# Transposing by the whole array in even head steps and by two row tiles in odd ones, with the weighted sum turned back three steps late

## The chip, the cores and the metric

One core of a Trainium2 chip runs the whole program. Its engines are PE (TensorE: MATMUL, and PEld for its weight loads), DVE (VectorE), ACT (ScalarE), POOL (GpSimd) and SP (SyncE, which issues the DMAs). The metric is the device time of one execution in microseconds (us), lower being better; the median of three runs is taken.

## What is computed

The program has six stages over 128 rows of 256 numbers, each added to a residual behind a layer norm. The change lies in the first, a cross attention over 12544 context rows with 16 heads of 64:

```python
q = x1 @ Wq
kv = x2 @ Wkv
k, v = jnp.split(kv, 2, axis=-1)
...
attn = jnp.einsum('bhid,bhjd->bhij', q, k) * SCALE
attn = jax.nn.softmax(attn, axis=-1)
out = jnp.einsum('bhij,bhjd->bhid', attn, v)
...
return out @ Wo + bo
```

The other stages (a banded attention, a mixture of 8 experts, a cross attention with relu keys, a state scan, and a mixture of 32 experts) stay as they are.

## The kernel before, in words

`stage_context` goes over the context in 14 chunks of 896 rows (`CK`, seven blocks of 128), and in each over 16 heads: 224 head steps `u`, in one loop on every engine. The order of the work is written out by hand, engine by engine, and held together by semaphores; each engine runs its own list in order. Keys and values are never stored whole: they are projected as the heads need them. Products that must be exact are split in a high and a low part (`Kh`, `Kl`; `cTh`, `cTl`), and three products of the parts are summed.

What PE does in step `u`, in this order (lines of the kernel before):

1. waits for the exponential of step u (`exp_done`), for `pTl_ready` of step u-1 and for `u_added`, and transposes the 128x896 tile `prob` into `pT_ps`, banks 4 and 5 of PSUM (L669 to L673). It works in two row tiles: rows 0 to 63 of `prob` go through one half of the array into bank 4, rows 64 to 127 through the other half into bank 5, with 14 transposes of 64 rows, two at a time;
2. from u = 2 on, `turn_sums(u - 2)` (L598 to L602): waits until DVE has added the two halves of the weighted sum into `osb` (`o_added`) and transposes it, again in two row tiles, into columns 448 to 511 of the banks 4 and 5 (`O_ps`), and signals `p_turned`;
3. in odd steps, `scores` (L587 to L596) of the next two heads: 12 matmuls in two row tiles, since a head has 64 numbers;
4. in steps of `v_steps` (all but u % 8 = 6, and not the last eight), `values` (L577 to L585): 6 matmuls of 128x512 into bank 6, for the values of a later group of heads. In six of the last eight steps `later_keys` stands in their place (keys of stage four);
5. `piece(u + 4)` (L563 to L575): 6 matmuls of 128x448 into bank 7, half the keys of a pair of heads, four steps ahead. It waits for `kl_ready` of the piece before;
6. `weighted_sum(u - 1)` (L604 to L618): 7 matmuls of 128x256 into bank 6 (`OT_ps`), with the values as weights and the high and low parts of the transposed probabilities as moving data.

All in 3, where it runs, and in 1 and 2 works by row tiles; all in 4 to 6 works by the whole array.

ACT copies `pT_ps` to the high part of `pT` (L427), copies the values (L435), forms the exponential of step u+1 (L402, L404) and copies the keys (`Kh`, L395). DVE subtracts for the low parts (L525 for `pT`, L463 for `Kl`), takes the maxima of the scores (L470), adds the turned sum to `U` (`update_sums`, L485, behind `p_turned`), updates `den` (L533) and adds the two halves of the weighted sum (`add_parts`, L478, behind `pv_done`), in this order:

```python
if u >= 2:
    update_sums(u - 2)
...
if u >= 1:
    add_parts(u - 1)
```

POOL splits the values, SP loads a chunk every 16 steps. Behind the last step the rest of the sums is turned, scaled (`scale_sums`), transposed by `turn_heads` (L633, whole array) and multiplied with `Wo` (L638).

The transposes of `norm_tensor` (L115) and those of `stage_relu_context` (L1359) work by the whole array too.

Of the kernel before, what the change touches and what calls it, by code (L numbers as in the profile page):

```python
# [17 lines left out]
F32 = mybir.dt.float32  # L18
# [4 lines left out]
ALU = mybir.AluOpType  # L23
# [3 lines left out]
P = 128  # L27
# [153 lines left out]
def stage_context(nc, t, sb, sem, link, ps, norms, v):  # L181
# [17 lines left out]
    with ExitStack() as keep:  # L199
# [12 lines left out]
        pT = [sb(f"pT{i}", [P, NT, 2, P], F32R, keep) for i in range(2)]  # L212
        osb = sb("osb", [P, P], F32, keep)
        nm = sb("nm", [P, 2, H0], F32, keep)
# [19 lines left out]
        pT_ps = ps[:, 4:6, 0:HK].rearrange("p s (t q) -> p s t q", q=P // 2)  # L234
        O_ps = ps[:, 4:6, HK:512]
        OT_ps = ps[:, 6, 0:2 * P]
        halves = (slice(0, DH0), slice(DH0, P))
# [20 lines left out]
        def v_low(g, i):  # L258

            return V[g % 2][:, i, :, DH0:P]  # L260

        def by_row(x):

            return x.rearrange("p t (s q) -> p s t q", s=2)
# [5 lines left out]
        with nc.Block() as block:  # L270
# [111 lines left out]
            def _(act):  # L382
# [70 lines left out]
            def _(dve):  # L453
# [22 lines left out]
                def add_parts(u):  # L476
                    dve.wait_ge(sem("pv_done"), u + 1)
                    nc.vector.tensor_reduce(osb[:, :], OT_ps.rearrange("p (a q) -> p q a", a=2), AX_X,  # L478
                                            ALU.add).then_inc(sem("o_added"), 1)
# [40 lines left out]
                for u in range(steps):  # L520
                    h, b = u % H0, u % 8
                    if 1 <= u and u - 1 + AHEAD < steps:
                        low_parts(u - 1 + AHEAD)
                    dve.wait_ge(sem("pTh_ready"), u + 1)
                    nc.vector.tensor_tensor(by_row(pT[u % 2][:, :, 1, :]), pT_ps,  # L525
                                            by_row(pT[u % 2][:, :, 0, :]).bitcast(F32), ALU.subtract).then_inc(sem("pTl_ready"), 1)
# [10 lines left out]
                    if u >= 1:  # L537
                        add_parts(u - 1)
                    if u >= steps - H0 + 3 and u % 2 == 1:
                        scale_sums((u - (steps - H0) - 3) // 2)  # L540
                update_sums(steps - 2)
# [7 lines left out]
            def _(pe):  # L549
# [48 lines left out]
                def turn_sums(u):  # L598
                    pe.wait_ge(sem("o_added"), u + 1)
                    for s, rows in enumerate(halves):  # L600
                        mm = nc.tensor.transpose(O_ps[:, s, :], osb[rows, :], ident[rows, rows])  # L601
                    return mm  # L602

                def weighted_sum(u):  # L604
                    h, g = u % H0, u // HG
                    pe.wait_ge(sem("pTl_ready"), u + 1)
                    if u >= 1:
                        pe.wait_ge(sem("o_added"), u)
# [53 lines left out]
                for u in range(steps):  # L662
                    h, g = u % H0, u // HG
                    pe.wait_ge(sem("exp_done"), u + 1)
                    if u >= 1:
                        pe.wait_ge(sem("pTl_ready"), u)
                    if u >= 3:
                        pe.wait_ge(sem("u_added"), u - 2)
                    for k in range(NT):  # L669
                        for s, rows in enumerate(halves):  # L670
                            mm = nc.tensor.transpose(pT_ps[:, s, k, :],  # L671
                                                     prob[:, :, :].rearrange("p a n -> p (a n)")[rows, k * P:(k + 1) * P],
                                                     ident[rows, rows])  # L673
                    if u >= 2:
                        mm = turn_sums(u - 2)
                    mm.then_inc(sem("p_turned"), 1)
                    if u % 2 == 1 and u + 1 < steps:
                        pe.wait_ge(sem("kl_ready"), u + 3)
                        scores((u + 1) // 2)
                    if u in v_steps:  # L680
                        j = v_steps.index(u)
                        gn, i = g + 1, V_AT.index(u % HG)
                        if j == 0:
                            pe.wait_ge(sem("first_vl"), NT)
                        else:
                            pe.wait_ge(sem("vraw_ready"), j)
                        if u >= 2:
# [16 lines left out]
                    if u >= 1:  # L704
                        if u in v_steps:
                            pe.wait_ge(sem("vraw_ready"), v_steps.index(u) + 1)
                        if u in later_at:
                            pe.wait_ge(sem("dkT_ready"), later_at.index(u) + 1)
                        weighted_sum(u - 1)
                    if u == steps - 1:  # L710
# [1172 lines left out]
```

## Time and profile before

| | |
|---|---|
| median of 3 runs | 1496.01 us (1495.39 to 1496.62) |
| the profiled execution | 1500.16 us |
| its span, first to last instruction | 1498.3 us |
| mean granted clock of TensorE | 0.983 of 2.4 GHz |
| PE busy | 1442.7 us, 96% |
| PEld busy | 1228.0 us, 82% |
| DVE busy | 1070.5 us, 71% |
| ACT busy | 827.8 us, 55% |
| POOL busy | 607.0 us, 41% |

The profile is of one execution. Busy time is the union of an engine's instructions; matmuls are pipelined, and their ends are modelled, so one matmul's row overlaps the next one's, and starts say more than ends. A row of a timeline gives start, length of the whole group, engine, line, operation, what is written and read, the shapes and how many instructions; in brackets how long the engine had stood idle, and for what. Head steps of `stage_context` run from 31.7 to 1143 us, three quarters of the whole span.

### The profile page before, as it was taken

What the parts mean: (1) busy time and instruction counts of PE and PEld (TensorE: products, weight loads), DVE (VectorE), ACT (ScalarE), POOL (GpSimd) and SP (SyncE); (2) the same over time, 40 slices, a digit from 0 to 9 for tenths busy, and PEclk for the clock granted to TensorE, in tenths of its full rate; (3) what the DMA queues carried; (4) which work ended last, traced back from release to release, by engine and by line L of the source; (5) the groups of instructions that cost most, each with busy time, mean ns of one, the idle gap of its engine ahead of it and who ended that gap; (6) DMA issues with size and microseconds to landing.
All of it is one profiled execution on the core that took longest, in us unless ns stands there. A gap on an engine that the chain in (4) does not pass through costs nothing. (4 is left out here: it accounts for less than half of the span.)

```text
span 1498.3 us, 28535 instructions
## 1 busy us (share of the span) xinstructions
PE 1442.7 (96%) x11057; PEld 1228.0 (82%) x11057; DVE 1070.5 (71%) x2051; ACT 827.8 (55%) x1578; POOL 607.0 (41%) x524
## 2 busy tenths in 40 slices
PE   8999999999999999999999999999998889999678
PEld 7888888888888888888888888888886879998558
DVE  5777777777777777777777777777785646677774
ACT  4666666666656666666666666666662236666221
POOL 4353434435343435353434343443420327765330
PEclk9999999999999999999999999999999799999889
DMA  5000000000000000000000000000013502111810
GB/s 190 2 25 2 1 26 1 26 1 26 1 26 1 26 2 26 2 26 2 26 2 25 2 6 21 1 26 1 1 54 132 200 23 87 56 59 35 340 74 4
DMA packets 11257, 59.41 MB, mean 40 GB/s; under 512 B 2346, under 2 KB 4723, under 8 KB 10100
## 3 DMA queue, kind: packets, MB, share of 16 engines
q1 hardware_dynamic: 11124, 57.59, 10.4%
q8 instruction: 89, 1.46, 0.4%
q14 instruction: 44, 0.36, 0.1%
HBM read 57.45 MB, written 0.13 MB: 38 GB/s over the span
## 5 line engine op out<-in xcount | busy, mean ns | idle before, releaser
L525 DVE TENSOR_TENSOR pT<-ps,pT 128x896 fp32r<-128x896 f32 x224 | 244.5, 1092 | 174.7 <-ACT pT L427 174.7
L344 POOL CAST V<-Vraw 128x512 fp32r<-128x512 f32 x189 | 115.5, 611 | 619.0 <-ACT Vraw L435 515.5
L427 ACT ACTIVATE pT<-ps 128x896 fp32r<-128x896 f32 x224 | 206.0, 920 | 152.3 <-PE ps L601 152.0
L435 ACT COPY Vraw<-ps 128x512 f32<-128x512 f32 x189 | 110.8, 586 | 263.8 <-PE ps L582 263.8
L345 POOL TENSOR_TENSOR V<-Vraw,V 128x512 fp32r<-128x512 f32 x189 | 242.2, 1281 | 15.1
L470 DVE TENSOR_REDUCE nmx<-ps 128x1 f32<-128x896 f32 x224 | 242.1, 1081 | 0.0
L615 PEld LDWEIGHTS ps<-pT,V 128*128 128x128 f32 x1568 | 215.8, 189 | 10.7 <-ACT d_kT L411 2.4
L404 ACT ACTIVATE prob<-ps,nm 128x896 f32<-128x896 f32 x224 | 224.2, 1001 | 0.0
L615 PE MATMUL ps<-pT,V 128*128 128x256 f32 x1568 | 221.1, 280 | 1.4 <-ACT d_kT L411 1.4
L478 DVE TENSOR_REDUCE osb<-ps 128x128 f32<-128x256 f32 x224 | 95.1, 424 | 101.0 <-PE ps L615 99.3
L671 PE MATMUL ps<-ident,prob 64*128 64x64 f32 x3136 | 145.8, 230 | 4.1 <-ACT prob L404 2.6
L582 PE MATMUL ps<-wvh,cTh 128*128 128x512 f32 x392 | 143.2, 446 | 1.2 <-DVE V L515 1.2
L671 PEld LDWEIGHTS ps<-ident,prob 64*128 64x128 f32 x3136 | 115.2, 139 | 34.6 <-ACT prob L404 5.3
L463 DVE TENSOR_TENSOR Kl<-ps,Kh 128x448 fp32r<-128x448 f32 x224 | 137.6, 615 | 1.8 <-ACT Kh L395 1.8
L571 PE MATMUL ps<-cTh,wkh 128*128 128x448 f32 x448 | 130.8, 373 | 7.5 <-DVE Kl L463 7.5
L571 PE MATMUL ps<-cTh,wkl 128*128 128x448 f32 x448 | 128.5, 368 | 0.0
L571 PE MATMUL ps<-cTl,wkh 128*128 128x448 f32 x448 | 127.9, 367 | 0.0
L582 PE MATMUL ps<-wvh,cTl 128*128 128x512 f32 x392 | 122.9, 395 | 0.0
L582 PE MATMUL ps<-wvl,cTh 128*128 128x512 f32 x392 | 122.0, 393 | 0.0
L395 ACT CAST Kh<-ps 128x448 fp32r<-128x448 f32 x224 | 118.6, 529 | 1.2 <-PE ps L571 1.2
L571 PEld LDWEIGHTS ps<-cTh,wkh 128*128 128x128 f32 x448 | 82.2, 189 | 27.5 <-DVE Kl L463 11.2
L582 PEld LDWEIGHTS ps<-wvh,cTh 128*128 128x128 f32 x392 | 58.6, 188 | 41.9 <-issue 33.5
(319 smaller groups left out, 2478.7 us busy)
## 6 DMA issues: line engine op xcount, KB each, us to landing
raw<-in_ctxT SPq DMA_DIRECT2D x16, 896.0 KB, 4.6
d_raw<-in_ctxT SPq DMA_DIRECT2D x12, 896.0 KB, 4.7
w<-in_w SPq DMA_DIRECT2D x2, 4096.0 KB, 18.0
wg<-in_wg SPq DMA_DIRECT2D x1, 4352.0 KB, 17.3
wu<-in_wu SPq DMA_DIRECT2D x1, 4352.0 KB, 26.9
wd<-in_wd SPq DMA_DIRECT2D x1, 4352.0 KB, 37.1
e_ea<-in_alog SPq DMA_DIRECT2D x1, 2048.0 KB, 7.4
d_mrow<-in_mask SPq DMA_DIRECT2D x14, 112.0 KB, 4.6
```

The source lines that it names most:

```text
L344: link(pool, nc.gpsimd.tensor_copy(v_high(g, i), by_head(Vraw[:, j % 2, :])), "pool_chain")
L345: nc.gpsimd.tensor_tensor(v_low(g, i), by_head(Vraw[:, j % 2, :]), v_high(g, i).bitcast(F32), ALU.subtract).then_inc(sem("v_split"), 1)
L395: nc.scalar.copy(Kh[:, slot, cols], ps[:, piece_bank(p), 0:HK]).then_inc(sem("kh_ready"), 1)
L404: nc.scalar.activation(prob[:, :, :], S[u % 2], ACT.Exp, bias=nm[:, par, h:h + 1], scale=1.0, accum_out=rs[:, b:b + 1]).then_inc(sem("exp_ ...
L427: nc.scalar.activation(by_row(pT[u % 2][:, :, 0, :]), pT_ps, ACT.Copy).then_inc(sem("pTh_ready"), 1)
L463: nc.vector.tensor_tensor(Kl[:, slot, cols], ps[:, piece_bank(p), 0:HK], Kh[:, slot, cols].bitcast(F32), ALU.subtract).then_inc(sem("kl_re ...
L470: nc.vector.tensor_reduce(nmx[:, :], S[u % 2], mybir.AxisListType.XY, ALU.max, negate=True).then_inc(sem("chunk_max"), 1)
L525: nc.vector.tensor_tensor(by_row(pT[u % 2][:, :, 1, :]), pT_ps, by_row(pT[u % 2][:, :, 0, :]).bitcast(F32), ALU.subtract).then_inc(sem("pT ...
L571: mm = nc.tensor.matmul(ps[:, piece_bank(p), 0:HK], w[:, k, m * P:(m + 1) * P], x[:, k, half * HK:(half + 1) * HK], start=(n == 0), stop=( ...
L582: mm = nc.tensor.matmul(ps[:, bank, :], x[:, k, i * P:(i + 1) * P], w[:, k, cols], start=(n == 0), stop=(n == 3 * KT - 1))
L615: mm = nc.tensor.matmul(OT_ps, V[g % 2][:, k, h % HG, :], pT[u % 2][:, k, :, :].rearrange("p a q -> p (a q)"), start=(k == 0), stop=(k == ...
L671: mm = nc.tensor.transpose(pT_ps[:, s, k, :], prob[:, :, :].rearrange("p a n -> p (a n)")[rows, k * P:(k + 1) * P], ident[rows, rows])
```

## The change

Three things are changed, all in `stage_context`.

- In even steps `prob` is transposed by the whole array: 7 transposes of 128x128 into `pT_whole`, which is the same two banks seen as 896 columns in a row, and the turned sum goes to the 128 columns behind them (`O_whole`). ACT's copy and DVE's subtraction read that layout in even steps. Odd steps keep their two row tiles. `by_tiles(w)` says in which way the sum of step w is turned, which is that of step w + 3.
- The weighted sum of step w is turned in step w + 3 instead of w + 2, and DVE's `update_sums(u - 3)` stands in step u where `update_sums(u - 2)` stood. `osb` has two buffers for this (the halves of `xn`). In the last step the sums of two steps are turned and added.
- Waits of PE are left out or replaced: `turn_sums` waits for `o_added` in the last three sums only; ahead of the transposes `u_added` stands in place of `pTl_ready` and `u_added`; `scores` no longer waits for `kl_ready`, nor `values` for `vraw_ready`, nor `weighted_sum` for `pTl_ready`, in the steps where another wait covers it.

The core of the diff:

```diff
@@ -210,7 +210,7 @@
-        osb = sb("osb", [P, P], F32, keep)
+        osb = [v["xn"][:, i * P:(i + 1) * P] for i in range(2)]
@@ -233,6 +233,9 @@
         O_ps = ps[:, 4:6, HK:512]
+        whole = ps[:, 4:6, :].rearrange("p b n -> p (b n)")
+        pT_whole = whole[:, 0:CK].rearrange("p (t q) -> p t q", q=P)
+        O_whole = whole[:, CK:CK + P]
@@ -258,6 +261,10 @@
+        def by_tiles(w):
+            return (w + 3) % 2 == 1 or w + 3 >= steps
@@ -424,7 +431,10 @@
-                    nc.scalar.activation(by_row(pT[u % 2][:, :, 0, :]), pT_ps, ACT.Copy).then_inc(sem("pTh_ready"), 1)
+                    if u % 2 == 1:
+                        nc.scalar.activation(by_row(pT[u % 2][:, :, 0, :]), pT_ps, ACT.Copy).then_inc(sem("pTh_ready"), 1)
+                    else:
+                        nc.scalar.activation(pT[u % 2][:, :, 0, :], pT_whole, ACT.Copy).then_inc(sem("pTh_ready"), 1)
@@ -475,14 +485,16 @@
                 def update_sums(u):
                     h, b = u % H0, u % 8
-                    dve.wait_ge(sem("p_turned"), u + 3)
-                    sums = U[:, h, :].rearrange("p (s c) -> p s c", s=2)
-                    nc.vector.scalar_tensor_tensor(sums, sums, al[:, b:b + 1], O_ps,
+                    dve.wait_ge(sem("p_turned"), u + 4)
+                    sums, part = U[:, h, :], O_whole
+                    if by_tiles(u):
+                        sums, part = sums.rearrange("p (s c) -> p s c", s=2), O_ps
+                    nc.vector.scalar_tensor_tensor(sums, sums, al[:, b:b + 1], part,
@@ -522,11 +534,17 @@
-                    if u >= 2:
+                    if u >= 3:
+                        update_sums(u - 3)
+                    if u == steps - 1:
                         update_sums(u - 2)
@@ -596,15 +616,19 @@
                 def turn_sums(u):
-                    pe.wait_ge(sem("o_added"), u + 1)
+                    if u >= steps - 3:
+                        pe.wait_ge(sem("o_added"), u + 1)
+                    if not by_tiles(u):
+                        return nc.tensor.transpose(O_whole, osb[u % 2], ident[:, :])
@@ -662,28 +686,30 @@
                     pe.wait_ge(sem("exp_done"), u + 1)
-                    if u >= 1:
+                    if u >= 4:
+                        pe.wait_ge(sem("u_added"), u - 3)
+                    elif u >= 1:
                         pe.wait_ge(sem("pTl_ready"), u)
-                    if u >= 3:
-                        pe.wait_ge(sem("u_added"), u - 2)
                     for k in range(NT):
+                        if u % 2 == 0:
+                            mm = nc.tensor.transpose(pT_whole[:, k, :],
+                                                     prob[:, :, :].rearrange("p a n -> p (a n)")[:, k * P:(k + 1) * P],
+                                                     ident[:, :])
+                            continue
...
-                    if u >= 2:
-                        mm = turn_sums(u - 2)
+                    if u >= 3:
+                        mm = turn_sums(u - 3)
@@ -706,6 +732,9 @@
+                        if u == steps - 1:
+                            pe.wait_ge(sem("u_added"), u - 2)
+                            turn_sums(u - 2).then_inc(sem("p_turned"), 1)
                         weighted_sum(u - 1)
```

What PE has between the weighted sums of an even step, before (L615 the weighted sum, L671 the transposes, L601 the turn, L582 the values):

```order
L615 MATMUL ps<-pT,V 128x256 [waits o_added,pTl_ready,vraw_ready]
L615 MATMUL ps<-pT,V 128x256 x6
L671 MATMUL ps<-ident,prob 128x64 [waits u_added,pTl_ready,exp_done]
L671 MATMUL ps<-ident,prob 128x64 x13
L601 MATMUL ps<-ident,osb 128x64 [waits o_added]
L601 MATMUL ps<-ident,osb 128x64
L582 MATMUL ps<-wvh,cTh 128x512 [waits o_added,vraw_ready]
```

and now, with the new lines (L639, L695, L622, L602):

```order
L639 MATMUL ps<-pT,V 128x256 [waits vraw_ready]
L639 MATMUL ps<-pT,V 128x256 x6
L695 MATMUL ps<-ident,prob 128x128 [waits u_added,exp_done]
L695 MATMUL ps<-ident,prob 128x128 x6
L622 MATMUL ps<-ident,xn 128x128
L602 MATMUL ps<-wvh,cTh 128x512 [waits cT_split,o_added]
```

Sixteen instructions became eight, and the turn has no wait of its own. In an odd step the sixteen stay (L700, L624), and only the waits differ, the turn's among them:

```order
L639 MATMUL ps<-pT,V 128x256 [waits o_added]
L639 MATMUL ps<-pT,V 128x256 x6
L700 MATMUL ps<-ident,prob 128x64 [waits u_added,exp_done]
L700 MATMUL ps<-ident,prob 128x64 x13
L624 MATMUL ps<-ident,xn 128x64 x2
L613 MATMUL ps<-Kh,qh 128x448 x2
```

In the last step PE now has, between the transposes and the bias product (L742), one turn more ahead of the weighted sum:

```order
L700 MATMUL ps<-ident,prob 128x64 x13
L624 MATMUL ps<-ident,xn 128x64 x2
L1472 MATMUL ps<-cTh,d_wxh 128x448 [waits dkT_ready,vraw_ready,o_added]
L1472 MATMUL ps<-cTh,d_wxh 128x448
L1472 MATMUL ps<-cTh,d_wxl 128x448 x2
L1472 MATMUL ps<-cTl,d_wxh 128x448 x2
L624 MATMUL ps<-ident,xn 128x64 [waits o_added,u_added,dkT_ready]
L624 MATMUL ps<-ident,xn 128x64
L639 MATMUL ps<-pT,V 128x256 x7
L742 MATMUL ps<-brow,ones 128x256 [waits post_in,consts_ready]
```

The second L624 is the sum of step 221, which before was turned right behind the transposes of that step.

## Rows read from the trace of the kernel before

**Rows 1.** The page: busy time and share of each engine.

```profile
PE 1442.7 (96%) x11057; PEld 1228.0 (82%) x11057; DVE 1070.5 (71%) x2051; ACT 827.8 (55%) x1578; POOL 607.0 (41%) x524
```

**Rows 2.** Busy time by stretch: PE, PEld, DVE, ACT, POOL, clock, DMA share, GB/s.

```profile
600.00:700.00 100.00, 99.24 (x817) 83.61 (x814) 74.64 (x142) 60.93 (x118) 37.86 (x36) 1.00 0.03 11
```

**Rows 3.** An even step in order of time: start us, us, engine line op.

```profile
603.48 0.98 PE L615 MATMUL ps<-pT,V 128*128 128x256 f32 x7
...
604.02 0.20 ACT L404 ACTIVATION_READ_ACCUMULATOR prob<-ps,nm 128x1 f32 x1
...
604.39 0.65 PE L671 MATMUL ps<-ident,prob 64*128 64x64 f32 x14
604.50 0.42 DVE L478 TENSOR_REDUCE osb<-ps 128x128 f32<-128x256 f32 x1
...
604.98 0.28 PE L601 MATMUL ps<-ident,osb 64*128 64x64 f32 x2
```

**Rows 4.** The same timeline: values behind the even step, then the odd step.

```profile
605.18 0.73 PE L582 MATMUL ps<-wvh,cTh 128*128 128x512 f32 x2
...
605.75 0.63 PE L582 MATMUL ps<-wvh,cTl 128*128 128x512 f32 x2
...
606.88 0.59 ACT L435 COPY Vraw<-ps 128x512 f32<-128x512 f32 x1 [0.66 <-PE ps L582]
...
607.91 0.98 PE L615 MATMUL ps<-pT,V 128*128 128x256 f32 x7
...
608.82 0.65 PE L671 MATMUL ps<-ident,prob 64*128 64x64 f32 x14
...
609.41 0.27 PE L601 MATMUL ps<-ident,osb 64*128 64x64 f32 x2
...
609.49 0.45 PE L593 MATMUL ps<-Kh,qh 64*128 64x448 f32 x2
```

**Rows 5.** Timeline, the one step in eight without value products.

```profile
613.61 0.98 PE L615 MATMUL ps<-pT,V 128*128 128x256 f32 x7
...
614.97 0.61 DVE L463 TENSOR_TENSOR Kl<-ps,Kh 128x448 fp32r<-128x448 f32 x1
...
615.11 0.27 PE L601 MATMUL ps<-ident,osb 64*128 64x64 f32 x2
...
615.64 0.68 PE L571 MATMUL ps<-cTh,wkh 128*128 128x448 f32 x2 [0.26 <-DVE Kl L463]
...
616.15 0.56 PE L571 MATMUL ps<-cTl,wkh 128*128 128x448 f32 x2
```

**Rows 6.** The page: groups by line, how many, busy us and mean ns.

```profile
L615 PE MATMUL ps<-pT,V 128*128 128x256 f32 x1568 | 221.1, 280 | 1.4 <-ACT d_kT L411 1.4
```

**Rows 7.** Timeline, PE: transposes by the whole array in stage_relu_context.

```profile
1249.72 0.60 PE L1359 MATMUL ps<-ident,d_kT 128*128 128x128 f32 x4
1250.08 0.66 PE L1371 MATMUL ps<-d_kTh,d_qh 128*128 128x448 f32 x2
```

**Rows 8.** Timeline, PE: the same straight behind a weighted sum.

```profile
1122.69 1.09 PE L615 MATMUL ps<-pT,V 128*128 128x256 f32 x7
1123.63 0.60 PE L633 MATMUL ps<-ident,U 128*128 128x128 f32 x4
```

**Rows 9.** Timeline, PE: two transposes that waited for their input.

```profile
1149.01 0.44 PE L115 MATMUL ps<-ident,xn 128*128 128x128 f32 x2 [0.40 <-DVE xn L101]
```

**Rows 10.** Timeline, the last step of the stage.

```profile
1132.22 1.01 PE L671 MATMUL ps<-ident,prob 64*128 64x64 f32 x14
...
1134.33 1.09 DVE L525 TENSOR_TENSOR pT<-ps,pT 128x896 fp32r<-128x896 f32 x1 [1.58 <-ACT pT L427]
...
1135.76 1.08 PE L615 MATMUL ps<-pT,V 128*128 128x256 f32 x7 [0.72 <-ACT d_kT L411]
```

**Rows 11.** Busy time by stretch, with the granted clock (columns of rows 2).

```profile
1132.20:1133.30 1.10, 1.10 (x18) 0.96 (x17) 0.42 (x1) 0.00 (x0) 0.00 (x0) 0.50 0.00 0
1248.90:1250.10 1.20, 1.20 (x14) 1.14 (x11) 0.00 (x0) 0.94 (x2) 1.20 (x2) 1.00 0.00 0
```

More of the change, by code:

```diff
@@ L477, in add_parts @@
                     dve.wait_ge(sem("pv_done"), u + 1)
-                    nc.vector.tensor_reduce(osb[:, :], OT_ps.rearrange("p (a q) -> p q a", a=2), AX_X,
+                    nc.vector.tensor_reduce(osb[u % 2], OT_ps.rearrange("p (a q) -> p q a", a=2), AX_X,
                                             ALU.add).then_inc(sem("o_added"), 1)
@@ L524, in _ @@
                     dve.wait_ge(sem("pTh_ready"), u + 1)
-                    nc.vector.tensor_tensor(by_row(pT[u % 2][:, :, 1, :]), pT_ps,
-                                            by_row(pT[u % 2][:, :, 0, :]).bitcast(F32), ALU.subtract).then_inc(sem("pTl_ready"), 1)
+                    high, low = pT[u % 2][:, :, 0, :], pT[u % 2][:, :, 1, :]
+                    if u % 2 == 1:
+                        high, low, turned = by_row(high), by_row(low), pT_ps
+                    else:
+                        turned = pT_whole
+                    nc.vector.tensor_tensor(low, turned, high.bitcast(F32), ALU.subtract).then_inc(sem("pTl_ready"), 1)
                     if u % 2 == 1 and u + 1 < steps:
                         max_step(u + 1)
-                    if u >= 2:
+                    if u >= 3:
+                        update_sums(u - 3)
+                    if u == steps - 1:
                         update_sums(u - 2)
@@ L538, in _ @@
                         add_parts(u - 1)
-                    if u >= steps - H0 + 3 and u % 2 == 1:
-                        scale_sums((u - (steps - H0) - 3) // 2)
+                    if u >= steps - H0 + 4 and u % 2 == 0:
+                        scale_sums((u - (steps - H0) - 4) // 2)
+                    if u == steps - 1:
+                        scale_sums(PAIRS - 2)
                 update_sums(steps - 2)
@@ L598, in turn_sums @@
                 def turn_sums(u):
-                    pe.wait_ge(sem("o_added"), u + 1)
+                    if u >= steps - 3:
+                        pe.wait_ge(sem("o_added"), u + 1)
+                    if not by_tiles(u):
+                        return nc.tensor.transpose(O_whole, osb[u % 2], ident[:, :])
                     for s, rows in enumerate(halves):
-                        mm = nc.tensor.transpose(O_ps[:, s, :], osb[rows, :], ident[rows, rows])
+                        mm = nc.tensor.transpose(O_ps[:, s, :], osb[u % 2][rows, :], ident[rows, rows])
                     return mm
@@ L605, in weighted_sum @@
                     h, g = u % H0, u // HG
-                    pe.wait_ge(sem("pTl_ready"), u + 1)
-                    if u >= 1:
+                    if u == steps - 1:
+                        pe.wait_ge(sem("pTl_ready"), u + 1)
+                    if u >= 1 and (u == steps - 1 or not (u + 1 in v_steps or u + 1 in later_at)):
                         pe.wait_ge(sem("o_added"), u)
@@ L664, in _ @@
                     pe.wait_ge(sem("exp_done"), u + 1)
-                    if u >= 1:
+                    if u >= 4:
+                        pe.wait_ge(sem("u_added"), u - 3)
+                    elif u >= 1:
                         pe.wait_ge(sem("pTl_ready"), u)
-                    if u >= 3:
-                        pe.wait_ge(sem("u_added"), u - 2)
                     for k in range(NT):
+                        if u % 2 == 0:
[3 more added lines that the diff above has]
+                            continue
                         for s, rows in enumerate(halves):
@@ L673, in _ @@
                                                      ident[rows, rows])
-                    if u >= 2:
-                        mm = turn_sums(u - 2)
+                    if u >= 3:
+                        mm = turn_sums(u - 3)
                     mm.then_inc(sem("p_turned"), 1)
                     if u % 2 == 1 and u + 1 < steps:
-                        pe.wait_ge(sem("kl_ready"), u + 3)
                         scores((u + 1) // 2)
@@ L684, in _ @@
                             pe.wait_ge(sem("first_vl"), NT)
-                        else:
-                            pe.wait_ge(sem("vraw_ready"), j)
                         if u >= 2:
@@ L708, in _ @@
                             pe.wait_ge(sem("dkT_ready"), later_at.index(u) + 1)
+                        if u == steps - 1:
+                            pe.wait_ge(sem("u_added"), u - 2)
+                            turn_sums(u - 2).then_inc(sem("p_turned"), 1)
                         weighted_sum(u - 1)
```

## The prediction

> **What bounds the kernel now.** I read the page first: PE is busy for 96% of the span, DVE for 71% [rows 1]. Then one stretch of the stage that the diff touches: from 600 to 700 us PE is busy for 99.24 of 100 us at a granted clock of 1.00, DVE for 74.64, ACT for 60.93 [rows 2]. So PE is the bound, and what a change is worth is read from the starts of its instructions: the end of a matmul row overlaps the next instruction, so I take the last start of a row as its start plus its length less the mean of one instruction.
>
> *An even step* [rows 3]. The weighted sum (L615) starts at 603.48; seven in 0.98 at 0.28 each [rows 6] put the last start, which I call W, at 604.18, and the distance between two at (0.98 - 0.28) / 6 = 0.117. The row-tiled transposes (L671) start at 604.39, so 0.21 after W instead of 0.117. The exponential they read had ended at 604.02 + 0.20 = 604.22, so it was not what held them: the gap lies between whole-array and row-tiled work. Seven pairs in 0.65, at 0.22 for one matmul, are 0.43 from first to last start. The two pieces of the weighted sum's turn (L601) start at 604.98, 0.16 after the last pair, and not 0.06 as the pairs do among themselves (0.43 / 7). DVE had added `osb` from 604.50 to 604.92: that is the wait. The values (L582) follow at 605.18, and their second matmul at 605.18 + 0.73 - 0.39 = 605.52, 0.34 behind the first, where the usual distance is 0.63 - 0.39 = 0.24, or 0.23 before rounding [rows 4]. From W to that second matmul: 1.34 us.
>
> *An odd step* [rows 4]. W is 607.91 + 0.70 = 608.61; transposes at 608.82, last pair at 609.25, L601 at 609.41, again 0.16 later; the scores follow 0.08 after it, with no gap, for they are row-tiled too.
>
> *One step in eight*, with u % 8 = 6, has no value products [rows 5]. W is 614.31. PE is through with L601 at 615.11, then waits for DVE's `Kl`, which ends at 614.97 + 0.61 = 615.58, and L571 starts at 615.64, 1.33 after W. That `Kl` stands behind the add of the same weighted sum on DVE, so it hangs on W and not on the transposes.
>
> **The change part by part.**
>
> *The turn three steps late.* The turn of step u-3 reads an `osb` that was added a whole step before, and a second `osb` (a half of `xn`) lets DVE write the next one. The wait for `o_added` ahead of L601 goes: 0.16 becomes 0.06, so 0.10 a step. What is late next? PE now waits for `u_added` ahead of the transposes instead; DVE does that update 1.2 us or more earlier, and its place in DVE's order does not change. In odd steps all of this is on PE's path: 111 odd steps have a turn; the one at u = 221 is held by an exponential. 110 x 0.10 = **11.0 us less**. Behind L601 the scores keep their distance.
>
> *Whole-array transposes in even steps.* Fourteen tiled and two tiled become seven and one. The trace has such transposes elsewhere: four in 0.60 at 0.27 each [rows 7] are 0.11 apart, 0.109 before rounding. They are costlier than the pairs (0.06). What they save is the two switches. Entry: L633 starts 0.12 after the last start of L615 (1123.63 against 1122.69 + 1.09 - 0.28 = 1123.50, a rounded 0.13), no gap [rows 8]. But the exponential now holds them: it ends 0.04 after W, and the one release that I can read, `Kl` to L571, takes 0.06 at most [rows 5]; with 0.05 the first is at W + 0.09. After a wait the second follows by 0.44 - 0.27 = 0.17 [rows 9], then six more by 0.109: the eighth starts at W + 0.91. Exit: the last L1359 starts at 1250.05, the second matmul behind it at 1250.08 + 0.66 - 0.37 = 1250.37, so 0.32 later where its kind is 0.20 apart: 0.12 over [rows 7]. For values that is 0.23 + 0.12 = 0.35. Sum: 0.91 + 0.35 = 1.26 against 1.34, 0.08 less. Bounds: without the exponential's wait 0.88 + 0.35 = 1.23, 0.11 less; with a release 0.04 longer, 0.04 less. Even steps with values number 81, three more near the end have key products in their place: 84 x 0.08 = **6.7 us less** (3.4 to 9.2). The Trainium skill, "TensorEngine Tiling (Array Packing)", Key Properties, says that a change of tiling mode drains TensorE, which agrees with the 0.21; its Theoretical Speedup gives row tiling up to 2x at a contraction of 64 or less, which speaks against this part. At that factor a whole transpose would take twice a pair, 0.124, and the even steps would lose 0.04 each, which would end at 1488.7 us; the 0.109 of rows 7 decides against it.
>
> *Steps without values.* Whole or tiled, PE is done before W + 1.33, where `Kl` comes: 27 x 0.
>
> *What comes later.* In an even step the last transpose starts at W + 0.91, and before the last L601 at W + 0.80, so ACT's copy of `pT` begins 0.11 later. ACT then sits idle for 0.66 before it takes the values [rows 4], so this is covered; at a slip over 0.66 the exponential would follow. At u = 220, where nothing stands between, it costs 0.11. DVE has the same instructions in the same order. No DMA moves, nor anything on SP or POOL.
>
> *The end.* In the last step one more turn stands ahead of the weighted sum, and waits for the update of step 220, behind DVE's `pT` that ends at 1134.33 + 1.09 = 1135.42 [rows 10]. With 0.34 of update it comes at about 1135.7, where PE started its sum at 1135.76: only the turn itself and its switch stay, **0.3 us more**, with the 0.1 of u = 220 inside the rounding.
>
> **The sum.** -11.0 - 6.7 + 0.3 = -17.4 us. The profiled execution took 1500.16 us (span 1498.3), 4.15 over the median of the runs, 1496.01; it would come to 1482.8, and the median to **1478.6 us**.
>
> **The rivals.**
>
> *The even steps give nothing.* For it: exponential and `Kl` both stand within 0.1 us of PE there. Against it: rows 3 leave 0.08. Then 1496.0 - 11.0 + 0.3 = 1485.3 us. Chance 0.14.
>
> *It gives more*: the exponential doesn't hold the whole transposes, 84 x 0.11 = 9.2, or `Kl` comes earlier in 27 steps. 1476.1 us or a little lower. Chance 0.08.
>
> *Slower: the gaps stay, and come from another cause.* If the 0.21 and the 0.34 belong to a change between the operand types of transposes and products, not to row tiles, whole transposes pay both and the longer pass: first at W + 0.21, eighth at 0.21 + 0.17 + 0.65 = 1.03, exit 0.20 + 0.34, together 1.57 against 1.34. 84 x 0.23 = 19.3 more, less 11.0: 1496.0 + 8.6 = 1504.6 us. It decides from 11 / 84 = 0.13 a step on. Rows 7 and 8 show neither gap. Chance 0.04.
>
> *Slower by the clock.* In the stretch of the last step the granted clock is 0.50 (1.2 GHz) and fourteen pairs take 1.01 instead of 0.65 [rows 10, 11]. Would the even steps fall to that level in their transposes, 84 x 0.36 = 30 more, 1478.6 + 30 = 1509 us. Against it, a stretch of 14 matmuls that are nearly all whole transposes runs at 1.00 (2.4 GHz) behind dense products [rows 11]. The Trainium skill, "TensorE: Matmul & The Clock Gate", Part 4, says that transposes do not count as activity for the full clock in the same way; by that rule this rival would come, and the trace does not bear it out. Chance 0.02.
>
> *The change doesn't do what it says*: the late turn meets another wait of the same length. Then only the even steps gain, 1489.6 us. Chance 0.03.
>
> **How the numbers follow.** The forecast's chance is 0.69. Its own bounds are 1476.1 to 1481.9, with the even steps' term from 9.2 to 3.4. The range takes in the rival of empty even steps and a little of the larger gain: 1474 to 1486, which leaves out the slower cases, the late wait, and the outer tails. Some 0.2% of the time, 3 us, is what a measurement of this kernel can tell from no change; no case lies within it but in its tails. Faster 0.93, same 0.01, slower 0.06, where the tails of the late-wait case make the 0.01.
>
> **What would show it.** In the profile after: the turn (two tiled pieces) 0.06 behind the last pair in odd steps; eight whole transposes in even steps 0.11 apart, the first about 0.09 after W; the second value matmul 1.26 after W; from W to W the even step shortened from 4.43 to 4.35 and the odd one from 5.70 to 5.60 [rows 3 to 5], and in those without values L571 still 1.33 after W. It would be wrong if PE idled ahead of the whole transposes by more than 0.1 us, if their distance were above 0.12, if the granted clock in the stage fell under 1.00, or if ACT's copy came so late that the exponential slid behind the weighted sum.

## The result, and the profile after

The changed kernel took 1477.51 us in the median of four runs (1474.21 to 1478.98), the kernel before 1496.32 (four runs). The ratio is 0.9866, 95% interval [0.984, 0.9891]: 1.3% faster, by about 19 us, which is clear of the noise. A ratio is worked out from the single runs and not from the two medians. The forecast was 1478.6.

The page of the changed kernel, where L695 is the whole-array transpose, 784 of them at 0.28 us:

```profile
PE 1420.6 (96%) x10163; PEld 1234.9 (84%) x10163; DVE 1072.7 (73%) x2051; ACT 827.4 (56%) x1578; POOL 608.5 (41%) x524
...
L695 PE MATMUL ps<-ident,prob 128*128 128x128 f32 x784 | 108.4, 279 | 2.7 <-ACT prob L411 2.7
```

and its busy time from 600 to 700 us (PE, PEld, DVE, ACT, POOL, clock, DMA share, GB/s):

```profile
600.00:700.00 100.00, 99.48 (x757) 86.46 (x754) 76.11 (x145) 61.66 (x119) 38.26 (x37) 1.00 0.03 10
```

PE is still the bound, at a granted clock of 1.00 in this stretch, as in [rows 2].

The timeline of an even step, as [rows 3] show it of before. The weighted sum is L639, the turn L622, the values L602:

```profile
594.45 0.98 PE L639 MATMUL ps<-pT,V 128*128 128x256 f32 x7
...
594.99 0.20 ACT L411 ACTIVATION_READ_ACCUMULATOR prob<-ps,nm 128x1 f32 x1
...
595.27 0.96 PE L695 MATMUL ps<-ident,prob 128*128 128x128 f32 x7
...
596.07 0.27 PE L622 MATMUL ps<-ident,xn 128*128 128x128 f32 x1
...
596.09 0.71 PE L602 MATMUL ps<-wvh,cTh 128*128 128x512 f32 x2
596.38 0.92 ACT L437 ACTIVATE pT<-ps 128x896 fp32r<-128x896 f32 x1 [0.76 <-PE ps L622]
```

W, the last start of the weighted sum, is 594.45 + 0.70 = 595.15. The whole transposes start 0.12 behind it, the turn at W + 0.92, the second value matmul at 596.09 + 0.71 - 0.39 = 596.41, so W + 1.26, which is the forecast's number against 1.34 before. ACT's copy of `pT` (L437) starts 1.23 after W; before it was 605.29 - 604.18 = 1.11.

An odd step, as [rows 4]. The row-tiled transposes are L700, the turn L624, the scores L613:

```profile
598.81 0.98 PE L639 MATMUL ps<-pT,V 128*128 128x256 f32 x7
...
599.72 0.65 PE L700 MATMUL ps<-ident,prob 64*128 64x64 f32 x14
599.83 0.43 DVE L488 TENSOR_REDUCE xn<-ps 128x128 f32<-128x256 f32 x1 [0.97 <-PE ps L639]
...
600.21 0.23 PE L624 MATMUL ps<-ident,xn 64*128 64x64 f32 x2
...
600.24 0.45 PE L613 MATMUL ps<-Kh,qh 64*128 64x448 f32 x2
```

W is 599.51. The transposes start at W + 0.21 as before; the turn comes 0.70 behind W instead of 0.80, before DVE is through with its add at 600.26, and the scores come 0.03 behind the turn, where it was 0.08.

A step without value products, as [rows 5], and the odd step behind it:

```profile
604.36 0.98 PE L639 MATMUL ps<-pT,V 128*128 128x256 f32 x7
...
605.15 0.75 PEld L695 LDWEIGHTS ps<-ident,prob 128*128 128x128 f32 x7
...
605.72 0.61 DVE L473 TENSOR_TENSOR Kl<-ps,Kh 128x448 fp32r<-128x448 f32 x1
...
606.39 0.68 PE L591 MATMUL ps<-cTh,wkh 128*128 128x448 f32 x2
...
607.24 1.09 DVE L542 TENSOR_TENSOR pT<-ps,pT 128x896 fp32r<-128x896 f32 x1 [0.90 <-ACT pT L437]
...
607.72 0.98 PE L639 MATMUL ps<-pT,V 128*128 128x256 f32 x7
608.17 0.20 ACT L411 ACTIVATION_READ_ACCUMULATOR prob<-ps,nm 128x1 f32 x1
608.24 0.34 DVE L497 SCALAR_TENSOR_TENSOR U<-U,al,ps 128x128 f32<-128x128 f32 x1
...
608.73 0.65 PE L700 MATMUL ps<-ident,prob 64*128 64x64 f32 x14
```

L591 waits for `Kl` and starts at 606.39, 1.33 after W (605.06): unchanged. But the odd step behind starts its transposes 0.31 after its W (608.42), not 0.21. The exponential had ended at 608.37; DVE's update of `U` ended at 608.58, and PE waits for `u_added`.

The distances from W to W, the medians of the steps 16 to 207 over PE's starts:

| step | before | after | difference |
|---|---|---|---|
| even, with values | 4.43 | 4.35 | -0.07 |
| odd, behind an even one with values | 5.70 | 5.55 | -0.15 |
| u % 8 = 6, without values | 3.35 | 3.35 | 0.00 |
| u % 8 = 7, behind that | 5.70 | 5.66 | -0.04 |

In eight steps that is 3 x 0.074 + 3 x 0.149 + 0.042 = 0.71 us, and 28 times that is 19.9 us. The measure that I use below is the loop: from the start of PE's first transpose of `prob` to DVE's add into `res` at the end of the stage. It went from 1114.6 to 1094.4 us, 20.2 less. It is read from one profiled execution of each kernel, and so is every step below.

The sum of the steps and the loop agree to 0.3 us, but two things at the end of the stage hide in that. The first is a gain that no one had asked for. With the later turn, `scale_sums` moved too, in DVE's list, from the odd steps of the last sixteen to the even ones. Before, it stood once between the add of a weighted sum and the `Kl` that PE waits for:

```profile
1088.83 0.62 DVE L463 TENSOR_TENSOR Kl<-ps,Kh 128x448 fp32r<-128x448 f32 x1
...
1089.50 0.68 PE L571 MATMUL ps<-cTh,wkh 128*128 128x448 f32 x2 [0.88 <-DVE Kl L463]
```

W of this step (u = 214) is 1087.55, so L571 started 1.95 after it and not 1.33. This step took 3.98 us before and takes 3.36 now. The second is the clock. In the last steps PE stands idle for up to 2.7 us, and then the granted clock is 0.50 for a while in both kernels ([rows 11] for before; 0.50 from 1107.90 to 1109.70 now). What runs in that while takes longer, here the whole transposes of step 222, 1.76 us instead of 0.96:

```profile
1107.92 1.76 PE L695 MATMUL ps<-ident,prob 128*128 128x128 f32 x7 [2.71 <-ACT prob L411]
```

Where the lower clock falls differs from kernel to kernel: step 222 takes between 6.4 and 8.9 us in the eleven traces, 8.37 before and 8.58 in the changed kernel. So a difference of a us or less between two loops says little by itself, and the steps decide.

### The profile page after: what moved, and what is told of

The parts are those of the page before. It is cut to its first block and busy times, and to the rows that moved or that the text cites. A ratio compares the mean times of both kernels' runs of the same rounds, so it can differ in the third digit from the quotient of the medians.

```text
span 1475.1 us, 26352 instructions
## 1 busy us (share of the span) xinstructions
PE 1420.6 (96%) x10163; PEld 1234.9 (84%) x10163; DVE 1072.7 (73%) x2051; ACT 827.4 (56%) x1578; POOL 608.5 (41%) x524
## 3 DMA queue, kind: packets, MB, share of 16 engines
q8 instruction: 81, 1.33, 0.4%
## 5 line engine op out<-in xcount | busy, mean ns | idle before, releaser
L639 PEld LDWEIGHTS ps<-pT,V 128*128 128x128 f32 x1568 | 214.9, 188 | 9.2 <-ACT d_kT L418 1.1
L639 PE MATMUL ps<-pT,V 128*128 128x256 f32 x1568 | 220.0, 280 | 0.7 <-ACT d_kT L418 0.7
L488 DVE TENSOR_REDUCE xn<-ps 128x128 f32<-128x256 f32 x224 | 95.0, 424 | 81.3 <-PE ps L639 81.3
L437 ACT ACTIVATE pT<-ps 128x896 fp32r<-128x896 f32 x112 | 103.0, 919 | 85.8 <-PE ps L622 84.9
L602 PE MATMUL ps<-wvh,cTh 128*128 128x512 f32 x392 | 141.2, 442 | 1.1 <-DVE V L527 1.1
L591 PE MATMUL ps<-cTh,wkh 128*128 128x448 f32 x448 | 131.1, 374 | 4.4 <-ACT wkh L393 0.6
L591 PE MATMUL ps<-cTl,wkh 128*128 128x448 f32 x448 | 128.7, 368 | 0.4 <-DVE cTl L511 0.4
L591 PE MATMUL ps<-cTh,wkl 128*128 128x448 f32 x448 | 128.5, 368 | 0.5 <-DVE wkl L514 0.5
L602 PE MATMUL ps<-wvh,cTl 128*128 128x512 f32 x392 | 122.8, 394 | 0.0
L602 PE MATMUL ps<-wvl,cTh 128*128 128x512 f32 x392 | 121.7, 391 | 0.0
L695 PE MATMUL ps<-ident,prob 128*128 128x128 f32 x784 | 108.4, 279 | 2.7 <-ACT prob L411 2.7
L591 PEld LDWEIGHTS ps<-cTh,wkh 128*128 128x128 f32 x448 | 81.8, 188 | 27.0 <-DVE Kl L473 10.2
L613 PE MATMUL ps<-Kh,qh 64*128 64x448 f32 x448 | 93.0, 405 | 0.0
```

The lines of the kernel that those rows point to most:

```text
L591: mm = nc.tensor.matmul(ps[:, piece_bank(p), 0:HK], w[:, k, m * P:(m + 1) * P], x[:, k, half * HK:(half + 1) * HK], start=(n == 0), stop=( ...
L602: mm = nc.tensor.matmul(ps[:, bank, :], x[:, k, i * P:(i + 1) * P], w[:, k, cols], start=(n == 0), stop=(n == 3 * KT - 1))
L639: mm = nc.tensor.matmul(OT_ps, V[g % 2][:, k, h % HG, :], pT[u % 2][:, k, :, :].rearrange("p a q -> p (a q)"), start=(k == 0), stop=(k == ...
L695: mm = nc.tensor.transpose(pT_whole[:, k, :], prob[:, :, :].rearrange("p a n -> p (a n)")[:, k * P:(k + 1) * P], ident[:, :])
```

## The experiments

Their times carry some us of noise from other stages (last section), so each is given with its loop, read from the same starts in its trace:

| kernel | median, us | ratio to before, 95% interval | loop, us |
|---|---|---|---|
| before | 1496.32 | | 1114.6 |
| changed | 1477.51 | 0.9866 [0.984, 0.9891] | 1094.4 |
| late_only | 1468.39 | 0.9809 [0.9774, 0.9843] | 1084.3 |
| whole_only | 1492.38 | 0.9966 [0.995, 0.9983] | 1106.6 |
| waits_back | 1479.89 | 0.9886 [0.9857, 0.9916] | 1094.3 |
| whole_all | 1523.64 | 1.0179 [1.0126, 1.0232] | 1141.2 |
| tiles_at_6 | 1476.51 | 0.9847 [0.9831, 0.9863] | 1090.2 |
| kl_first | 1479.70 | 0.9864 [0.9842, 0.9885] | 1093.6 |
| tiles_at_6_kl_first | 1471.66 | 0.9812 [0.9797, 0.9826] | 1086.2 |
| late_held | 1501.15 | 1.0009 [0.9985, 1.0034] | 1116.5 |
| late_kl_first | 1462.86 | 0.9774 [0.9742, 0.9805] | 1080.9 |

Each ratio is to runs of the kernel before on the same chip, so compare ratios and not the medians of two rows. whole_all and kl_first have two runs each. One of the eight executions of late_held took 5836.85 us; its ratio leaves that one out, and nothing on record says why it was so long.

### late_only: the late turn without whole transposes

```diff
+        def tiled(u):
+
+            return True
+
         def by_tiles(w):
 
-            return (w + 3) % 2 == 1 or w + 3 >= steps
+            return tiled(w + 3) or w + 3 >= steps
...
-                        if u % 2 == 0:
+                        if not tiled(u):
                             mm = nc.tensor.transpose(pT_whole[:, k, :],
```

and the same in ACT's copy and DVE's subtraction: every step works by row tiles, and the turn stays three steps late.

> The late turn alone: every step keeps its two row tiles. My theory: the turn 0.06 behind the last pair in all steps. Odd steps go from 5.70 to 5.55 us as in the changed kernel (0.15 less, 111 of them), even ones with values from 4.43 to 4.33 (0.10 less, 84), those without values stay at 3.35, and the step behind them no longer waits for u_added. Sum about -25 us against the kernel before, so about 1471 us and 4 to 5 us below the changed kernel. Rival: the odd steps' 0.15 needs the whole-array step ahead of it (a switch less in the pair); then odd steps give 0.10 and the sum is -19 us, 1477 us.

It took 1468.39 us, with a loop 10.1 us shorter than that of the changed kernel. An even step of it (L643 the weighted sum, L704 transposes, L628 the turn, L606 values):

```profile
588.43 0.98 PE L643 MATMUL ps<-pT,V 128*128 128x256 f32 x7
...
589.34 0.65 PE L704 MATMUL ps<-ident,prob 64*128 64x64 f32 x14
...
589.83 0.23 PE L628 MATMUL ps<-ident,xn 64*128 64x64 f32 x2
...
589.98 0.73 PE L606 MATMUL ps<-wvh,cTh 128*128 128x512 f32 x2
```

W is 589.13. The turn starts at W + 0.70, and the values follow it after 0.15, where it was 0.20 before [rows 3, 4]; the second value matmul comes at 589.98 + 0.73 - 0.39 = 590.32, W + 1.19, against 1.26 with whole transposes. From W to W the even steps take 4.28 us, where 4.33 was expected, the odd ones 5.55, the step behind one without values 5.55 too. So this half of the change alone is worth 30.3 us of the loop (0.6 of it the moved `scale_sums`), where 25 was expected, and the other half, put on top of it, costs 10.1: 0.07 in each of the 84 even steps, which is 5.9, and 0.105 in the 28 steps with u % 8 = 7, which is 2.9. The other 1.3 lies mostly in the last steps, 0.8 of it in step 222, where the clock is 0.50 in both kernels and the whole transposes take 1.76 us against 1.01 for tiled ones.

### whole_only: whole transposes without the late turn

```diff
+            return (w + 2) % 2 == 1 or w + 2 >= steps
...
                     if u >= 2:
                         mm = turn_sums(u - 2)
```

The kernel before, with whole transposes in even steps and one `osb`.

> The whole-array transposes alone: even steps as in the changed kernel, the turn two steps late as before, one osb. My theory: the eighth whole transpose comes 0.91 after W, later than osb is added (0.77 to 0.80), so the even steps gain 0.075 as in the changed kernel (84 x 0.075 = 6.3 us), the odd ones stay at 5.70; the step behind those without values loses up to 0.1 (27 x). So -3.6 to -6.3 us, about 1491 us. Rival: the gain of the even steps hangs on the late turn; then 1496 us.

The loop is 8.0 us shorter than before. An even step (L633 the weighted sum, L617 the turn, L598 values):

```profile
600.68 0.98 PE L633 MATMUL ps<-pT,V 128*128 128x256 f32 x7
...
601.70 0.42 DVE L488 TENSOR_REDUCE osb<-ps 128x128 f32<-128x256 f32 x1
...
602.30 0.27 PE L617 MATMUL ps<-ident,osb 128*128 128x128 f32 x1
...
602.33 0.71 PE L598 MATMUL ps<-wvh,cTh 128*128 128x512 f32 x2
```

DVE ends its add at 602.12, W (601.38) + 0.74, and the turn comes at W + 0.92: the eight whole transposes are long enough to cover the wait that the tiled ones ran into. Even steps take 4.34 us, odd ones 5.69. The loss expected in the step behind one without values did not come (5.70, as before): its transposes start 0.33 after W there, but its turn stands at W + 0.80 as before, since it waits for DVE's add anyway. That makes the gain 8.0 and not the 3.6 to 6.3 expected. And the even steps are why the halves don't add up. Alone they take 30.3 and 8.0 us off the loop, together 20.2: in even steps both remove the same wait, and the whole transposes pay for it with a longer pass.

### late_held: the wait put back, with all else late

```diff
                 def turn_sums(u):
-                    if u >= steps - 3:
-                        pe.wait_ge(sem("o_added"), u + 1)
+                    pe.wait_ge(sem("o_added"), min(u + 2, steps - 2) if u < steps - 3 else u + 1)
```

on late_only.

> late_only (row tiles everywhere, turn three steps late), but each turn waits again for the add of the weighted sum of the step just before, as in the kernel before. It tells what the 0.15 us a step of late_only is made of. My theory: all of it is this one wait, 0.10 in which PE idles ahead of the turn and 0.05 behind it, since weights that were held back can't be loaded under the transposes ahead; then the steps are those of the kernel before (turn 0.80 after W, scores 0.08 and values 0.20 behind the turn, stage within 2 us of 1114.6). Rival: part of the gain comes from elsewhere (the waits left out ahead of the transposes and products, the second osb); then the scores stay 0.03 behind the turn, and the stage keeps at least 8 us of the 30.

The ratio is 1.0009, and the loop 1116.5 us. An even step (L642 the weighted sum, L703, L627, L606):

```profile
606.17 0.98 PE L642 MATMUL ps<-pT,V 128*128 128x256 f32 x7
...
607.08 0.65 PE L703 MATMUL ps<-ident,prob 64*128 64x64 f32 x14
607.18 0.42 DVE L492 TENSOR_REDUCE xn<-ps 128x128 f32<-128x256 f32 x1
...
607.66 0.28 PE L627 MATMUL ps<-ident,xn 64*128 64x64 f32 x2
...
607.87 0.73 PE L606 MATMUL ps<-wvh,cTh 128*128 128x512 f32 x2
```

The turn is back at W (606.87) + 0.79, just behind DVE's 607.60, and the values are back at 0.21 behind it; in odd steps the scores stand 0.09 behind the turn again. Even steps take 4.44 us and odd ones 5.71, 0.01 more than before. So the one wait for `o_added` makes the whole 0.15 us a step: 0.10 ahead of the turn and 0.05 behind it.

### waits_back: are fulfilled waits free?

```diff
                 def turn_sums(u):
-                    if u >= steps - 3:
-                        pe.wait_ge(sem("o_added"), u + 1)
+                    pe.wait_ge(sem("o_added"), u + 1)
...
+                        pe.wait_ge(sem("kl_ready"), u + 3)
                         scores((u + 1) // 2)
```

and the same for `pTl_ready` and `o_added` ahead of the weighted sum and `vraw_ready` ahead of the values, on the changed kernel. The waits ahead of the transposes stay as changed.

> The changed kernel with all the PE waits put back that the change left out: o_added ahead of each turn, kl_ready ahead of the scores, pTl_ready ahead of each weighted sum, vraw_ready ahead of the values. My theory: those are fulfilled long before, and the 0.05 by which scores follow the turn sooner than before (0.03 against 0.08) comes from a turn whose weights are no longer held back: same as the changed kernel within 1 us, scores 0.03 behind the turn. Rival: a wait on the instruction itself costs, even if it is fulfilled, the kl_ready ahead of the scores above all: scores 0.08 behind the turn, 111 x 0.05 = 5.5 us more than the changed kernel.

The loop is 1094.3 us, as in the changed kernel, and the scores stand 0.03 behind the turn. Waits that are fulfilled when PE comes to them cost nothing that shows here; the same even step reads 4.34 us in this trace and 4.355 in that of the changed kernel, so some 0.015 a step can't be told apart. With late_held this puts the 0.05 on a turn that had to wait, and not on the presence of waits; why its successor then starts later, I only argue: while the turn waits, no weights of it or behind it are loaded. The records fit: in the odd step above, the turn's first weight load starts at 600.15 and its matmul at 600.21, and in the step of [rows 3] both start at 604.98. No run changed that alone.

### whole_all: whole transposes in odd steps too

```diff
+        def tiled(u):
+
+            return False
...
-                        if u % 2 == 0:
+                        if not tiled(u):
                             mm = nc.tensor.transpose(pT_whole[:, k, :],
```

> Whole-array transposes in odd steps too. The array then switches from the turn to the scores, which work by row tiles: the turn 0.91 after W instead of 0.70, scores about 0.2 behind it instead of 0.03. So odd steps get longer by about 0.38 us: 111 x 0.38 = 42 us more than the changed kernel, about 1519 us. If the switch into the scores costs nothing (as 0.03 behind the turn), only 0.21 each, 1501 us.

The loop grew by 46.8 us over the changed kernel, where 42 was expected. An odd step of it (L643, L699, L626, and L617 the scores):

```profile
610.98 0.98 PE L643 MATMUL ps<-pT,V 128*128 128x256 f32 x7
...
611.80 0.94 PE L699 MATMUL ps<-ident,prob 128*128 128x128 f32 x7
...
612.58 0.27 PE L626 MATMUL ps<-ident,xn 128*128 128x128 f32 x1
...
612.78 0.47 PE L617 MATMUL ps<-Kh,qh 64*128 64x448 f32 x2
```

The turn comes 0.90 after W, and the scores, which work by row tiles, 0.20 behind it. Such a step takes 5.94 us instead of 5.55, and those with u % 8 = 7 take 6.15 instead of 5.66: 84 x 0.39 + 28 x 0.50 = 47 us. So a switch between whole array and row tiles shows here on the other side of the transposes, with the same 0.20. That the odd steps keep their tiles is right for this reason.

### tiles_at_6 and kl_first: the step without values and the one behind

```diff
+        def tiled(u):
+
+            return u % 2 == 1 or u % HG == HG - 2
+
         def by_tiles(w):
 
-            return (w + 3) % 2 == 1 or w + 3 >= steps
+            return tiled(w + 3) or w + 3 >= steps
```

(`HG` is 8), with `tiled(u)` in place of `u % 2 == 1` wherever the layout is chosen, and for kl_first and tiles_at_6_kl_first, in DVE's list:

```diff
-                    if 1 <= u and u - 1 + AHEAD < steps:
+                    if 1 <= u and u - 1 + AHEAD < steps and u % HG != HG - 2:
                         low_parts(u - 1 + AHEAD)
...
+                    if u % HG == HG - 3 and u + AHEAD < steps:
+                        low_parts(u + AHEAD)
                     if u >= 1:
                         add_parts(u - 1)
```

> The changed kernel, but steps with u % 8 = 6 (no value products) keep row tiles too. My theory: in the changed kernel the step behind them starts its transposes 0.31 after W instead of 0.21, since the whole transposes end later, so pT, its low part and the update of U come 0.1 later, and PE waits for u_added. With row tiles there this wait goes: 27 x 0.10 = 2.8 us less than the changed kernel, steps without values still 3.35 us (held by Kl). Rival: the 0.10 comes from the exponential or from elsewhere and stays: no difference.

> The changed kernel with the DVE order of tiles_at_6_kl_first, whole transposes in the steps without values. My theory: these steps get 0.15 shorter, but the next step waits for u_added already and its wait grows by as much: within 1 us of the changed kernel. Rival: 4 us less than the changed kernel.

> As tiles_at_6, and in the step before, DVE forms Kl ahead of the add of the weighted sum instead of behind it. My theory: PE waits for Kl in the steps without values only because of that order; Kl then ends about 1.13 after W instead of 1.28, so these steps go from 3.35 to 3.20 us: 27 x 0.15 = 4 us less than tiles_at_6, 7 us less than the changed kernel. Rival: the exponential or the update of U of the next step is late by then and takes the gain back: no more than 1 us less than tiles_at_6.

In tiles_at_6 the step behind the one without values (L643 the weighted sum, L704 transposes):

```profile
603.64 0.98 PE L643 MATMUL ps<-pT,V 128*128 128x256 f32 x7
...
603.93 0.34 DVE L501 SCALAR_TENSOR_TENSOR U<-U,al,ps 128x128 f32<-128x128 f32 x1
...
604.55 0.65 PE L704 MATMUL ps<-ident,prob 64*128 64x64 f32 x14
```

W is 604.34; `U` is updated by 604.27, where it was 0.16 after W in the changed kernel, and the transposes start 0.21 after W. That step takes 5.55 us instead of 5.66, which is the 2.8 us expected. The loop is 4.1 us shorter; the other 1.3 is 0.015 in each even step, which nothing in the edit explains. The ratio is 0.9847 against 0.9866, and the two intervals overlap: the runs alone would not have told it.

In kl_first the steps without values fall from 3.35 to 3.21 us, and the step behind them pays (L641, L702):

```profile
605.50 0.98 PE L641 MATMUL ps<-pT,V 128*128 128x256 f32 x7
...
606.16 0.34 DVE L497 SCALAR_TENSOR_TENSOR U<-U,al,ps 128x128 f32<-128x128 f32 x1
...
606.65 0.65 PE L702 MATMUL ps<-ident,prob 64*128 64x64 f32 x14 [0.17 <-DVE U L497]
```

W is 606.20, `U` is done at 606.50, and the transposes start at W + 0.45. That step takes 5.80 us instead of 5.66, and of the 0.14 gained nothing is left; the loop is 0.8 us shorter. With tiles in that step (tiles_at_6_kl_first) the same reordering takes 4.0 us off the loop.

### late_kl_first: the best of the parts

late_only with DVE's reordering.

> late_only with Kl formed ahead of the add in the steps before those without value products. If the gain of 0.146 us in 27 steps stands as it did over tiles_at_6: the loop 3.9 us shorter than late_only (stage from its first transposes to its end 1080.3 instead of 1084.3), about 1464.5 us, the fastest of all. Rival: with the shorter steps the update of U or the exponential is late in the step behind, and less than 1 us is left.

1462.86 us, ratio 0.9774 [0.9742, 0.9805] to the kernel before, the fastest here; the loop is 3.4 us shorter than late_only's. A step without values and the next (L645 the weighted sum, L706 transposes, L597 keys):

```profile
598.40 0.98 PE L645 MATMUL ps<-pT,V 128*128 128x256 f32 x7
...
599.60 0.62 DVE L477 TENSOR_TENSOR Kl<-ps,Kh 128x448 fp32r<-128x448 f32 x1
...
600.28 0.68 PE L597 MATMUL ps<-cTh,wkh 128*128 128x448 f32 x2 [0.26 <-DVE Kl L477]
...
601.61 0.98 PE L645 MATMUL ps<-pT,V 128*128 128x256 f32 x7
...
602.02 0.34 DVE L501 SCALAR_TENSOR_TENSOR U<-U,al,ps 128x128 f32<-128x128 f32 x1
...
602.52 0.65 PE L706 MATMUL ps<-ident,prob 64*128 64x64 f32 x14
```

`Kl` now ends 1.12 after W (599.10) instead of 1.27, and L597 starts 1.18 after it. In the step behind, `U` is updated by 602.36, just after W (602.31) and before the transposes at W + 0.21: nothing is given back.

## Why the prediction was right, and where its terms were off

**The bound and the place of the gain** stood: PE, in the seam between the weighted sum and what follows the turn.

**The odd steps.** Forecast: 110 x 0.10 = 11.0. Measured: 84 x 0.149 + 28 x 0.042 = 13.7. Two errors in opposite directions. The sentence that failed first is that "behind L601 the scores keep their distance": they come 0.05 sooner, and late_held shows that this belongs to the wait. The other is "DVE does that update 1.2 us or more earlier". I had read this from steps with values alone. In the trace of before, this is the step behind one without values:

```profile
617.38 0.34 DVE L485 SCALAR_TENSOR_TENSOR U<-U,al,ps 128x128 f32<-128x128 f32 x1
...
617.87 0.65 PE L671 MATMUL ps<-ident,prob 64*128 64x64 f32 x14
```

The update ended at 617.72, only 0.15 ahead of PE, which is the distance at which PE follows it now that it waits (608.58 to 608.73): there was no slack left. The whole transposes made it later by 0.1, and PE now waits for it; tiles_at_6 takes that wait away. "What comes later" looked for this slip at the exponential and found it covered, and did not follow it through DVE.

**The even steps.** Forecast: 0.08 each, 6.7 us. Measured: 0.074, 6.2 us. The steps of the sum were right too: the exponential, which ends 0.04 after W, holds the first weight load until W + 0.09 (605.15 in the step without values), the first transpose stands at W + 0.12 where I had 0.09, from the first to the seventh it is 0.96 - 0.28 = 0.68 where I had 0.17 + 0.55 = 0.72, and the eighth comes at W + 0.92 where I had 0.91. The size was right for the pair as changed, but the term is not what the whole transposes are worth. Against tiled transposes with a late turn they lose 0.07 a step (late_only), since the tiled turn gained 0.15 in even steps as well. I had compared with the step of before, in which the wait was part of what they replaced.

**The steps without values**: 27 x 0, as forecast, with L591 at W + 1.33, but for one. Step 214 gained 0.62 us. "DVE has the same instructions in the same order" was wrong: `scale_sums` had moved, and with it what stood ahead of `Kl`.

**The end**: +0.3 forecast. The added turn stands at 1116.58, 0.10 behind the update that it waits for, which ended at 1116.48. The weighted sum starts at 1116.79, 0.57 after the end of ACT's `d_kT` (1116.22), where it was 0.06 before. So PE lost about 0.5 there, but the step as a whole got 0.15 shorter, for its tiled transposes ran at the full clock now (0.65 us, and 1.01 before). What the term was worth can't be read from these two traces.

**The rivals.** "The even steps give nothing" fell: 0.074. "The gaps stay, and come from another cause" fell too: the 0.21 ahead of row-tiled transposes and the 0.20 between whole-array turn and tiled scores appear exactly where the tiling changes (whole_all), and are gone where it doesn't. The 0.34, though, was not from the row tiles: the second value matmul stands 0.32 behind the first in the changed kernel too (596.09 to 596.41), where nothing is tiled. That rival was right in this one part, and the forecast's exit of 0.35 had room for it. The clock stayed at 1.00 from 40 to 1100 us, in all steps but the last few; there it fell in the kernel before as well, behind idle time. So the rival that takes its rule from the Trainium skill, "TensorE: Matmul & The Clock Gate", Part 4, fell for this mix, in which products run between the transposes; what the rule says of transposes alone isn't tested by it. The Trainium skill, "TensorEngine Tiling (Array Packing)", Theoretical Speedup, gives tiling up to 2x where a dimension is 64 or less. Measured is 1.8: the whole transposes stand 0.109 apart behind the second, a pair of tiled ones 0.062.

**Slips that changed nothing.** With whole transposes 0.124 apart, the terms of the prediction give a loss of about 0.02 in each even step and some 1487 us, not 0.04 and 1488.7. The "fourteen pairs" of the clock's rival are fourteen transposes, seven pairs.

**What was luck.** The terms sum to -17.4 us, and the loop gave -20.2: 2.7 more in the odd steps, 0.6 in step 214, 0.5 less in the even ones, the rest at the end. That the median came within 1.1 us of the forecast is owed in part to the other stages, which vary by more than that from run to run (last section).

**What the forecast lacked** is the comparison of the halves. Its sum was right to 1.1 us in the median for the change as a whole, while one of its two parts was a loss of some 9 us in the steps beside the other.

## What to carry to other kernels

When a change has two parts that touch the same seam, price each against the other's result and not only against the kernel before: two parts that remove the same wait do not add up, and the dearer one can be a loss. A wait on the engine that bounds can cost more than its idle time, here 0.15 for 0.10, and it is likely, though only argued, that this is because what stands behind the waiting instruction can't be prepared; move what it waits for a step back rather than fill the gap. List what moved in every engine's order: `scale_sums` moved by one step and gave 0.6 us unasked. And a slip of a tenth of a microsecond has to be followed along every engine to its last reader, in the shortest step of the pattern, where the slack is least.

## What was not expected of the hardware

The remaining stages do the same work in all these kernels, and yet vary with the run, the second one most. That stage, from one add into `res` to the next, before and after (columns as above):

```profile
1146.28:1180.26 33.98, 29.49 (x150) 24.75 (x150) 19.66 (x40) 3.42 (x5) 2.46 (x2) 0.80 0.84 328
```

```profile
1127.33:1157.44 30.11, 24.98 (x150) 20.01 (x150) 19.65 (x40) 3.43 (x5) 2.46 (x2) 0.94 0.92 365
```

34.0 us at a mean granted clock of 0.80, and 30.1 us at 0.94, with PE busy for 29.5 and 25.0 us. In the profiled executions of the ten changed kernels it was 30.1 us in four, 31.7 in two and 33.7 to 34.05 in four. This alone is as large as some of the effects that were looked for. The span of the changed kernel's profiled execution is 23.1 us shorter than that of before: 20.2 by the loop, 3.9 by this stage, 0.3 by the rest behind it, less 1.3 by which the loop starts later. What sets which of them a run gets was not tried.
